# First weights' low parts moved from GpSimd to VectorE, and the first unit's samples loaded from two queues

## What is computed

```python
def _dense(x, wi_, wo_):
    return jax.nn.relu(x @ wi_) @ wo_

s0 = _dense(x, swi[0], swo[0])                 # swi[i]: 256 x 1024, swo[i]: 1024 x 256
s1 = _dense(x, swi[1], swo[1])
h = relu(einsum('bsd,bdf->bsf', x, wi[type_label]))
eo = einsum('bsf,bfd->bsd', h, wo[type_label])
gate_in = concatenate([eo[:, 0], s0[:, 0], s1[:, 0]], axis=-1)
w = softmax(relu(gate_in @ g1) @ g2, axis=-1)
x = x + eo * w0 + s0 * w1 + s1 * w2
x = x + (zX * lap_x(x) + zY * lap_y(x) + zR * x * (1 - x))   # reflecting borders
```

## Time and profile before

| | us |
|---|---|
| median of 3 runs | 1184.4 |
| lowest and highest of them | 1183.69 and 1185.29 |
| the profiled execution's own time | 1182.22 |
| its span, first to last instruction | 1180.4 |
| PE busy in the span | 1151.5 |
| DVE, ACT, POOL busy | 685.9, 455.3, 72.5 |

### The profile page before, as it was taken

The page is one execution under the profiler, slowest core; times in us unless marked ns, Lnnn a source line. Parts: engine busy times, 40 slices in busy tenths (PEclk is TensorE's granted clock), DMA queues, the critical chain, the costliest instruction groups (busy, mean ns, idle before and its releaser), DMA issues.

```text
span 1180.4 us, 16671 instructions
## 1 busy us (share of the span) xinstructions
PE 1151.5 (98%) x5996; PEld 979.1 (83%) x5996; DVE 685.9 (58%) x1008; ACT 455.3 (39%) x786; POOL 72.5 (6%) x105
## 2 busy tenths in 40 slices
PE   6999999999999999999999999999999999999995
PEld 4888888888889998888888888888888888888884
DVE  7655555555556763565465465465465566565564
ACT  3444444444546652333333333233233233333332
POOL 3101110111111210000000000000000000000001
PEclk9999999999999999999999999999999999999998
DMA  7644553444345753031230230230230230230200
GB/s 231 184 126 123 152 147 117 139 140 149 104 147 173 222 144 98 21 81 20 62 82 19 63 81 17 65 81 16 66 82 13 68 81 15 67 82 12 70 28 28
DMA packets 109410, 106.73 MB, mean 90 GB/s; under 512 B 78512, under 2 KB 85904, under 8 KB 109328
## 3 DMA queue, kind: packets, MB, share of 16 engines
q1 hardware_dynamic: 97088, 61.62, 18.8%
q0 software_dynamic: 12096, 44.05, 12.5%
q10 hardware_dynamic: 144, 0.00, 0.0%
HBM read 83.63 MB, written 17.56 MB: 86 GB/s over the span
## 4 chain that ended last, share of the span: by engine, by line
PE 94%; SPq 2%; DVE 2%; DMA 1%; issue 0%; ACT 0%; DVEq 0%; ACTq 0%
PE acc L767 31%; PE acc L768 16%; PE hbank L743 15%; PE hbank L742 15%; PE hbank L744 15%; PE tbank L699 1%; SPq L1006 1%; DMA xs<-in_x 0%; SPq L973 0%; DMA y<-y 0%; SPq L961 0%; PE tbank L700 0%; DMA rw<-in_x 0%; PE tbank L707 0%; PE acc L756 0%
## 5 line engine op out<-in xcount | busy, mean ns | idle before, releaser
L510 DVE SCALAR_TENSOR_TENSOR hl<-hbank,hh 128x512 fp32r<-128x512 f32 (+1 forms) x424 | 277.9, 656 | 431.5 <-ACT hh L837 431.4
L837 ACT ACTIVATE hh<-hbank 128x512 fp32r<-128x512 f32 (+1 forms) x424 | 240.9, 569 | 604.1 <-PE hbank L744 600.6
L767 PE MATMUL acc<-swo,hh 128*128 128x512 f32 x1024 | 370.9, 396 | 0.0
L768 PE MATMUL acc<-swo,hl 128*128 128x256 f32 x1024 | 286.7, 280 | 0.0
L767 PEld LDWEIGHTS acc<-swo,hh 128*128 128x128 f32 x1024 | 192.4, 188 | 45.5 <-DVE eo L528 0.2
L767 PE MATMUL acc<-ewo,hh 128*128 128x512 f32 x560 | 205.8, 398 | 2.7 <-DVE hl L510 2.5
L742 PE MATMUL hbank<-xh,swh 128*128 128x512 f32 x512 | 202.5, 396 | 0.0
L743 PE MATMUL hbank<-xl,swh 128*128 128x512 f32 x512 | 202.3, 395 | 0.0
L768 PEld LDWEIGHTS acc<-swo,hl 128*128 128x128 f32 x1024 | 193.2, 189 | 9.9
L744 PE MATMUL hbank<-xh,swl 128*128 128x512 f32 x512 | 199.2, 389 | 0.0
L768 PE MATMUL acc<-ewo,hl 128*128 128x256 f32 x560 | 157.6, 281 | 0.0
(11 more groups left out here) (167 smaller groups left out, 847.3 us busy)
## 6 DMA issues: line engine op xcount, KB each, us to landing
rw<-in_L_cond_wi POOLq DMA_DIRECT2D x42, 512.0 KB, 4.5
rw<-in_L_cond_wo POOLq DMA_DIRECT2D x42, 512.0 KB, 5.2
xs<-in_x SPq DMA_DIRECT2D x140, 64.0 KB, 3.0
eo_scratch<-eo SPq DMA_DIRECT2D x140, 64.0 KB, 2.4
xs<-in_x SPq DMA_DIRECT2D x16, 512.0 KB, 4.3
rw<-in_x SPq DMA_DIRECT2D x256, 32.0 KB, 2.2
ei<-eo_scratch SPq DMA_DIRECT2D x16, 512.0 KB, 5.4
out<-ot SPq DMA_DIRECT2D x15, 512.0 KB, 6.2
```

The source lines that it names most:

```text
L510: e.scalar_tensor_tensor(HL[:, g % NH, 0:w], bank[:, 0:w], 0.0, HH[:, g % NH, 0:w].bitcast(F32), ALU.max, ALU.subtract).then_inc(h_lo, 1)
L767: e.matmul(acc[j][:, 0:2 * D], HH[:, g % NH, js], woc[:, c, :], start=(c == 0), stop=False)
L768: m = e.matmul(acc[j][:, D:2 * D], HL[:, g % NH, js], woc[:, c, 0:D], start=False, stop=last)
L837: e.activation(HH[:, g % NH, 0:w], hbank[g % HRING][:, 0:w], ACT.Relu).then_inc(h_hi, 1)
```

## The change

Three things change.

1. `POOL_CUTS` is gone. POOL subtracts nothing any more; all low parts are DVE's and are counted on `w_lo`, in the same order as the high parts.
2. The chunks at which the shared sets' pieces and unit 0's pieces are cut are listed anew, at most one of these in a chunk. The two pieces that POOL had are cut at (0, 2), behind the sorting's last step there, and at (0, 4); piece (0, 1) moves from (0, 4) to (0, 5); pieces (1, 2) and (1, 3) move from pass 1, chunks 2 and 3, into the first unit, chunks 7 and 4. In chunk (2, 2), unit 0's piece 3 is now cut ahead of unit 1's piece 0.
3. Of unit 0's eight sample loads SP issues the four even ones; ACT issues the four odd ones in `first_samples`, after its cut at (0, 7).

```diff
-SHARED_CUTS = {(0, 0): (0, 0), (0, 2): (0, 2), (0, 4): (0, 1), (0, 6): (0, 3), (0, 7): (1, 0), (1, 1): (1, 1),
-               (1, 2): (1, 2), (1, 3): (1, 3)}
-UNIT_CUTS = {(1, 5): [(2, 0)], (1, 6): [(2, 2)], (2, 1): [(2, 1)]}
-POOL_CUTS = ((0, 0), (0, 2))
+FIRST_CUTS = {(0, 2): (0, 0), (0, 4): (0, 2), (0, 5): (0, 1), (0, 6): (0, 3), (0, 7): (1, 0), (1, 1): (1, 1), (1, 5): (2, 0),
+              (1, 6): (2, 2), (2, 1): (2, 1), (2, 2): (2, 3), (2, 4): (1, 3), (2, 7): (1, 2)}
 
 def cuts_at(n, c):
-    if (n, c) in SHARED_CUTS:
-        return [SHARED_CUTS[n, c]]
-    if (n, c) in UNIT_CUTS:
-        return UNIT_CUTS[n, c]
-    out = []
+    out = [FIRST_CUTS[n, c]] if (n, c) in FIRST_CUTS else []
     if 2 <= n < 1 + NU and c in (2, 3, 5, 6):
         out.append((n + 1, {2: 0, 3: 2, 5: 1, 6: 3}[c]))
-    if (n, c) == (2, 2):
-        out.append((2, 3))
     return out
...
+            def first_samples():
+                e.wait_ge(t_free, T_AT["rows"])
+                e.wait_ge(dve_seq, AT["samples"])
+                for b in range(1, 8, 2):
+                    e.reg_load(regs[b // 2], tab[0:1, 0, b:b + 1])
+                    v = e.snap(regs[b // 2], min_val=0, max_val=NS - 1)
+                    e.dma_start(XS[1][b:128:8, :, :], x[bass.ds(v, 1), :, :].rearrange("a (p j) d -> (a p) j d", p=16)) \
+                        .then_inc(x_in[1], 16)
...
+                if (n, c) == (0, NC - 1):
+                    first_samples()
...
-            for ws, p in POOL_CUTS:
-                hi, lo = cut_parts(ws, p)
-                e.wait_ge(w_hi, CUT_HI[ws, p])
-                e.tensor_tensor(lo, raw(ws, p), hi.bitcast(F32), ALU.subtract).then_inc(w_lo_pool, 1)
...
-            load_unit_x(0)
+            load_unit_x(0, range(0, 8, 2))
```

More of the change, by code:

```diff
@@ L137 @@
 CUT_HI = {k: i + 1 for i, k in enumerate(CUT_ORDER)}
-CUT_LO = {k: i + 1 for i, k in enumerate([k for k in CUT_ORDER if k not in POOL_CUTS])}
-CUT_LO_POOL = {k: i + 1 for i, k in enumerate(POOL_CUTS)}
+CUT_LO = CUT_HI
 def slots_of(u):
@@ L246, in cond_resid_program @@
         w_lo = sem("w_lo")
-        w_lo_pool = sem("w_lo_pool")
         xb_in = [sem(f"xb_in{i}") for i in range(2)]
@@ L300, in cut_done @@
         def cut_done(ws, p):
-            return (w_lo_pool, CUT_LO_POOL[ws, p]) if (ws, p) in POOL_CUTS else (w_lo, CUT_LO[ws, p])
+            return w_lo, CUT_LO[ws, p]
         def piece_src(a, b, p):
@@ L644, in _ @@
                     for ws, p in cuts_at(n, c):
-                        if (ws, p) not in POOL_CUTS:
-                            cut_low(ws, p)
+                        cut_low(ws, p)
                 if FIRST <= n < NP:
@@ L811, in _ @@
         def _(e):
+            regs = [e.alloc_register(f"first{k}") for k in range(4)]
             e.dma_start(itk[:], col(itok)).then_inc(itok_in, 16)
@@ L962, in table_value, with load_unit_x @@
                 return e.snap(regs[k], min_val=0, max_val=hi)
-            def load_unit_x(u):
+            def load_unit_x(u, part=None):
                 tile = 1 + u
@@ L970, in load_unit_x @@
                     e.wait_ge(t_prod, T_AT[tile_last(tile - 2)])
-                for b in range(k):
+                for b in part or range(k):
                     v = table_value(0, s0 + b, b % 4, NS - 1)
```

## The result

| | before | after |
|---|---|---|
| median (lowest to highest), us | 1184.43 (1183.69 to 1185.29) | 1175.32 (1174.12 to 1178.21) |
| ratio, 95% interval | | 0.9927 [0.9911, 0.9944] |
| the profiled execution's own time, span | 1182.22, 1180.4 | 1174.12, 1172.5 |

The changed kernel was timed twice more beside the kernel before: 0.9945 [0.9931, 0.9958], a gain of 7.0 us (1182.8 to 1175.83), and 0.9927 [0.9912, 0.9943], a gain of 8.3 us (1183.8 to 1175.48). Its 14 runs have a median of 1175.6. So the first comparison's gain of 9.1 us is the largest of three; the forecast was 6.5.

The account below looks back on a forecast made before the run. PE was taken as the bound, so the time follows the start of the first unit's matmuls. Transposes 6.05 us sooner plus 0.45 of clock gave 6.5 us, 1184.4 to 1177.9; range 1175.4 to 1181.0.

Parts of the forecast that it names:

- POOL's two subtractions: Start of pass 0: they hold up two small DVE instructions of 2.3 us each; without them sorting and table come 3.4 us sooner.
- The two pieces on DVE: Gate's passes: a low part costs DVE 1.22 us; at (0, 2) a 1.75 us gap before the table covers it.
- ACT's loads: Unit 0's samples: ACT starts with SP, at SP's 1.0 us a load; SP's last of four issued at 17.8.
- The rival of slow loads: ACT's four sample loads take over 1.75 us each; at 4 us a load the time is 1187; chance 0.04.
- The landing: Unit 0's samples ahead of the transposes at (1, 4): landings of 2.1 to 5.1 us, landed by 22.9 at the latest.
- POOL's pieces as hidden: Unit 0's four weight pieces on POOL start 3.4 us sooner, are needed only from (1, 5) on, and stay hidden.
- its sign that PE's wait would be gone or below 0.5 us: Ahead of PE's first transposes at (1, 4): the 3.1 us wait for `xs` disappears or falls below 0.5 us.
- Who is late next: At (1, 4): DVE's alternation sets PE's arrival at 24.3; transposes move there from 30.37, a gain of 6.05 us.
- full clock early: Rival in pass 0: fewer PE gaps raise the clock sooner; arrival 22.6, gain 8.2 us, time 1176.2; chance 0.17.
- The clock between transposes and first unit: Without PE's wait for `xs` the clock stays full up to the first unit's first matmul; gain some 0.45 us.
- Pass 2: Two cuts moved into the first unit cost nothing; at most both in full, 2.4 us.

Follow-up runs that it names:

- the hold: Changed kernel with POOL waiting for unit 0's samples to land before issuing unit 0's second weight piece; 1175.33 us, run again 1175.07 us.
- POOL late: Kernel before with POOL's two subtractions held until the table of samples is written; 1178.7 us, ratio 0.9966.
- the hold with the seven matmuls: Changed kernel with POOL's later weight pieces held until the samples landed and seven matmuls of ones ahead of PE's first work; 1173.97 us, again 1172.6 us.
- the cuts back: Changed kernel with the second shared set's two second-layer pieces cut at chunks 2 and 3 of pass 1 again; 1175.45 us, ratio 0.994.
- the seven matmuls: Changed kernel with seven matmuls of ones on PE ahead of its first work, product not used; 1175.39 us, ratio 0.9944.

## Why the prediction was right, and where its steps were not

The sign and the size held. The first median, 1175.32, lies 0.1 us under the range's low end of 1175.4, the median of all 14 runs 0.2 above it; the likeliest time, 1177.9, was 2.3 to 2.6 us too long. Point by point:

- *POOL's two subtractions*: right. The two instructions went to 0.17 us, as forecast (0.15), and the experiments showed the cause. (Only the first of the two is a cast; L377 is a scalar_tensor_tensor with both inputs in SBUF.) `hf` of (0, 0) and `msel` came 2.9 us sooner, not 3.41, since this execution's first input landed 0.5 us later (2.84 us; 2.33 in before's profile). The rule of the Trainium skill, "SBUF — State Buffer", section "Who interferes with whom", that the later of the two blocks for the whole instruction, fits DVE's 2.3 us rows at every place where they turned up. The same section of the Trainium skill has `copy`, `cast` and `tensor_scalar` among those that can contend, under conditions on their operands, and instructions with two SBUF inputs; the int32 `tensor_scalar` of 128x5 at 6.72 above was hit. POOL's row of 3.95 us shows less: POOL's start lies 0.53 us ahead of that of DVE's cut, yet POOL was the one lengthened, and the trace does not show which of the two had the ports first.
- *The two pieces on DVE*: right. The cut at (0, 2) ended at 13.18 as the table's first copy could start (13.10, two instructions overlapping at their ends); it cost 0.1 us at most. With the table's matmuls at full clock, done at 13.06, the gap of 1.75 us that was to cover it had just been used up.
- *ACT's loads*: right. Four in 3.56 us and a period of 1.0 us, SP's; the last of the eight went at 17.80, forecast 17.8. The rival of slow loads fell.
- *The landing*: the step that failed. The samples were put at "22.9 at the latest" from a longest landing of 5.1 us. In the new place the last took 6.24 us and landed at 24.04. POOL's weight pieces had moved up and together: before, the first three left at 18.99, 22.27 and 23.65, among loads issued over 7 us; now three leave at 15.41, 16.53 and 18.02, among loads issued over 3.2 us, and the DMA share of the window from 20 to 25 us is 1.05. The prediction kept the landing time of the looser traffic. It had named POOL's pieces as hidden, not as company for the samples. So its sign that PE's wait would be gone or below 0.5 us did not come true: 1.75 us were left, and they went where POOL's later pieces were held.
- *Who is late next*: also wrong, and in the other direction. PE came to (1, 4) at 22.42, not 24.3: the clock was full at the table, the rival "full clock early" (arrival 22.6, given 0.17), and `hf` of (1, 0) stood at 19.96, where the forecast had 21.84 and the rival 20.1. The two misses met at the same place: a start at 24.3 forecast, 24.18 found, through another bound. With the hold and an early clock the rival's full price shows: the first unit at 28.06, 8.45 us sooner than before, where it was put at 8.2.
- *The clock between transposes and first unit*: right in kind. The granted clock is 1.00 from 20 to 35 us; the second transposes take 0.55 instead of 0.90 us. From 24.18 to the first matmul 5.68 us, where 6.14 stood before: 0.46, forecast 0.45.
- *Pass 2*: right, nothing: the units keep 6.64 us from the first to the last.
- *What was not in the sum*: 1.3 us by the clock near 440 us. And the base: the forecast was set against a median 2.2 us above the profiled execution; the other medians of the kernel before were 1182.8 to 1183.8.

The predicted 6.5 us for the start of the first unit stands against 6.65 in the trace. As a sum it was right; as a chain of reasons it was right up to the loads' issue and then right by luck.

## What to carry to other kernels

Where an engine beside VectorE works out of SBUF at a moment when VectorE has a chain of small dependent instructions, look for small ones that take as long as the other's big one: giving that work to VectorE itself, in a gap of its chain, gained 3.5 us here together with the new list of cuts. When a chain of loads is moved up, list what else moves up with it and will travel beside it: the landing time of the old place (5.1 us at most here) need not hold with the traffic of the new one (6.24). And when a forecast start is hit, look whether it was hit by the bound that was named.

## What the runs showed of the hardware

- One POOL subtraction of 128x1024 held an instruction of DVE on a single partition for 2.35 us, and when both were large they lengthened each other: POOL's 2.35 us became 3.95, DVE's 1.22 became 2.97.
- Loads of 64 KB with three or more 512 KB pieces of POOL's queue beside them landed in up to 6.9 us, with one such piece in up to 5.0, with none in up to 2.6 (POOL late), the shortest of all in 2.0 to 2.2.
- PE's clock is not a function of the program alone. The same kernel had the table's four matmuls in 1.09 us in one execution and in 0.64 in another (the hold with the seven matmuls), with the same instructions ahead of them at the same times within 0.05 us. The Trainium skill, "TensorE: Matmul & The Clock Gate", Part 1, says that the low level's length at a kernel's start varies from run to run; these two rows agree, by the matmuls' lengths.
- Behind a gap of 2.1 to 3.0 us near 440 us the clock fell in seven profiles and stayed in six; between the profiles of before and after that was 1.3 us. The changed kernel's three profiles, the one with the cuts back and the one with the seven matmuls kept it, all four with the hold lost it, though no instruction near that place differs. Longer gaps lost it more often (2.51 to 2.96 us lost, 2.10 to 2.71 kept), but the two ranges overlap. What decides it stays open.
